# Cross-attention and two feed-forward layers in one kernel: the low half of an attention output tile taken by TensorE and ScalarE instead of VectorE

## The chip, the cores and the metric

The kernel runs on one NeuronCore of one Trainium2 chip. The metric is the device time of one execution in microseconds (us), the median of several runs. Five engines work side by side on one core: TensorE (PE in the profile, its weight loads PEld), VectorE (DVE), ScalarE (ACT), GpSimd (POOL) and SyncE (SP, which here only issues transfers). Each runs its own list of instructions in order, and they meet only at semaphores: a `wait_ge` on one engine blocks everything that is queued behind it on that engine.

## What is computed

The reference chains four blocks on 512 tokens (2 batches of 256) of width 512: a quantised product with the context, a mixture of 18 experts, a cross-attention with 32 heads on 8 key/value heads, and a gated low-rank layer. The change is in the cross-attention:

```python
q = (hidden_states @ q_proj_w.T).reshape(B, Q, NUM_HEADS, HEAD_DIM).transpose(0, 2, 1, 3)
...
scores = jnp.einsum('bhqd,bhkd->bhqk', q, k) * scale + attention_mask
attn = jax.nn.softmax(scores.astype(jnp.float32), axis=-1).astype(q.dtype)
out = jnp.einsum('bhqk,bhkd->bhqd', attn, v)
out = out.transpose(0, 2, 1, 3).reshape(B, Q, NUM_HEADS * HEAD_DIM)
return out @ o_proj_w.T
```

## The kernel before

**Numbers in two halves.** Every fp32 operand of a matrix product is held as two fp16 tensors, a high half (the value rounded to fp16) and a low half (the value minus the high half). `three_products` (L261 to L265) multiplies low by high, high by low and high by high into one PSUM bank, so each product of one 128-wide chunk is three matmuls of 128x512. Whoever produces an operand has to write both halves: typically ScalarE rounds (high) and GpSimd or VectorE subtracts (low).

**The attention stage.** The unit of work is a head tile `k`: one head, 128 query rows, 512 context columns. Four head tiles (`REP` = 4) that share one key/value head make an output tile `w` of 128 x 512, and four output tiles (`m` = 0 to 3) a group `g`; there are 8 groups (`KVH`), 32 output tiles and 128 head tiles. Each engine runs a function `attention(g, first)` over the 16 steps `j` of a group, once unrolled for group 0 and then as a hardware loop for groups 1 to 7:

- PE: `scores(k)` (3 matmuls) into one of the banks 0 to 3, having waited on `s_t` until head tile k-4 has left that bank; and in the same step one quarter of `values(w)` (3 matmuls) for the output tile three before, since its probabilities must have been exponentiated, normalised and transposed first. In group 0 there are values only in the last four steps. `values` writes into bank 6 or 7 by turns. At its first quarter it waits for the four transposes of its tile (`s_pT`) and, before the change, on `s_ol` until output tile w-2 has left the bank.
- DVE: `masked_scores` (L1374, PSUM to SBUF with the row maximum), `inverse_sum` of head tile k-1 (L1379), `prob_lo` of head tile k-2 (L1385, which waits for POOL's high half of the same tile), and once per output tile `o_lo` (L1390), the low half of the output, from PSUM and the high half.
- ACT: `exponentials` (L905), and once per output tile `o_hi` (L910), which rounds the output to fp16 into `q_sb`.
- POOL: `prob_hi` (L1092 on one column, then L1093 on 128x512), the high half of the probabilities. It waits for `inverse_sum` and, since the four slots of `hlr` are reused, for the transpose of head tile k-4.
- SP: `prob_transpose` (L325 to L331), one DMA transpose for each head tile, after `prob_lo`.

The order is written out by hand in these functions; there is no scheduler. After the loop PE finishes the values of output tiles 29, 30 and 31 with the output projection of group 0, `o_group(0)`, between the last two, and goes on with `o_group(1)` to `o_group(5)` and the last two projections.

`o_hi` and `o_lo` are what the change touches; before it they are

```python
def o_hi(w, mw):
    act.wait_ge(s_pv, w + 1)
    act.activation(q_sb[:, bass.ds(w, 1), 0, :], ps[6 + mw % 2][:, :], ACT.Copy, scale=1.0 / PSCALE).then_inc(s_oh, 1)
...
def o_lo(w, mw):
    dve.wait_ge(s_oh, w + 1)
    dve.scalar_tensor_tensor(out=q_sb[:, bass.ds(w, 1), 1, :], in0=ps[6 + mw % 2][:, :], scalar=1.0 / PSCALE,
                             in1=q_sb[:, bass.ds(w, 1), 0, :], op0=ALU.mult, op1=ALU.subtract).then_inc(s_ol, 1)
```

## Time and profile before

| | us |
|---|---|
| median of 3 runs | 716.15 (716.12 to 718.03) |
| the profiled execution | 715.52 |
| its span, first to last instruction | 713.7 |
| PE busy | 636.0 (89%) |
| DVE busy | 456.5 (64%) |
| POOL busy | 412.9 (58%) |
| ACT busy | 347.4 (49%) |
| granted TensorE clock, mean | 0.983 of full speed |

The span is shorter than the execution's time by 1.8 us that lie around it. Busy shares are means over stages with different limits: what bounds one stage is read from its own stretch of the trace. The attention stage lies between about 384 and 595 us of the span, the output projection and the last layer behind it.

### The profile page before, as it was taken

The numbers are of one execution on the slowest core, as the hardware profiler recorded it, in microseconds if no ns is written. First come the engines' busy times: TensorE is split into PE (matmuls) and PEld (weight loads), VectorE is DVE, ScalarE is ACT, GpSimd is POOL, SyncE is SP. The second block draws the span as 40 slices with busy tenths as digits, with TensorE's granted clock in tenths as the row PEclk, the third lists the DMA queues.
The fourth block names the chain that finished last, engine by engine and source line by source line (L and its number), as shares of the span: only waits on it lengthen the run. The fifth ranks groups of instructions, "written<-read, shape, count | busy, mean of one in ns | idle before, by whom it ended". The sixth has DMA issues, their size and how long they took to land.

```text
span 713.7 us, 12272 instructions
## 1 busy us (share of the span) xinstructions
PE 636.0 (89%) x3356; PEld 298.0 (42%) x3356; DVE 456.5 (64%) x1086; ACT 347.4 (49%) x706; POOL 412.9 (58%) x438
## 2 busy tenths in 40 slices
PE   5639999999999999999997778888888878999997
PEld 2214445444444444455553233333333333444453
DVE  5999886443444337544446999999999992000573
ACT  4415556533343323778777555565556552223122
POOL 4823233355455422677777878888888883538201
PEclk9959999999999999999999999999999999999999
DMA  8802000244444331121223998888888885134001
GB/s 328 336 0 74 1 0 0 91 133 147 132 124 138 120 133 60 60 104 74 90 86 93 168 166 163 161 162 162 162 162 161 162 162 121 59 118 176 1 1 60
DMA packets 149112, 83.04 MB, mean 116 GB/s; under 512 B 136762, under 2 KB 136890, under 8 KB 146141
## 3 DMA queue, kind: packets, MB, share of 16 engines
q1 hardware_dynamic: 146290, 77.90, 42.8%
q10 hardware_dynamic: 2795, 4.79, 2.2%
q8 instruction: 15, 0.25, 0.1%
q14 instruction: 12, 0.10, 0.0%
HBM read 48.03 MB, written 1.09 MB: 69 GB/s over the span
## 4 chain that ended last, share of the span: by engine, by line
PE 45%; DVE 20%; issue 17%; POOL 12%; DMA 2%; ACT 2%; DVEq 1%; POOLq 1%; SPq 0%; ACTq 0%
PE ps L263 15%; PE ps L265 14%; PE ps L264 14%; POOL hlr L1093 5%; POOL wsp L1013 4%; POOL hlr L1013 3%; DVE q_sb L1390 3%; DVE st L1136 1%; DVE f32r L1374 1%; PE ps L357 1%; DVE nw L1148 1%; DVE hlr L1385 1%; DVE nw L1147 1%; DVE f32r L1152 1%; DMA stage<-in_first_chunks 1%
## 5 line engine op out<-in xcount | busy, mean ns | idle before, releaser
L1013 POOL TENSOR_TENSOR wsp<-stage,wsp 128x512 f16<-128x512 f32 (+1 forms) x93 | 135.3, 1479 | 130.8 <-ACT wsp L744 68.5
L905 ACT ACTIVATE f32r<-f32r,mneg 128x512 f32<-128x512 f32 x128 | 92.4, 722 | 85.2 <-DVE mneg L1374 85.2
L1013 POOL TENSOR_TENSOR hlr<-f32r,hlr 128x512 f16<-128x512 f32 x52 | 61.2, 1178 | 100.0 <-ACT hlr L796 66.4
L1092 POOL TENSOR_SCALAR rinv<-rinv 128x1 f32<-128x1 f32 x128 | 83.1, 650 | 34.4 <-DVE rinv L1379 22.7
L1385 DVE SCALAR_TENSOR_TENSOR hlr<-f32r,rinv,hlr 128x512 f16<-128x512 f32 x128 | 95.6, 747 | 9.8 <-POOL hlr L1093 3.0
L1093 POOL TENSOR_SCALAR hlr<-f32r,rinv 128x512 f16<-128x512 f32 x128 | 92.7, 724 | 0.0
L1374 DVE CUSTOM_DVE_ANT_0 f32r<-ps,nmask 128x512 f32<-128x512 f32 x128 | 87.3, 683 | 0.0
L1293 DVE TENSOR_REDUCE ss<-f32r 128x4 f32<-128x512 f32 x48 | 32.9, 685 | 55.1 <-ACT f32r L785 55.0
L263 PE MATMUL ps<-q_sb 128*128 128x512 f16 x128 | 49.2, 385 | 9.0 <-POOL q_sb L1013 7.3
L1343 DVE SCALAR_TENSOR_TENSOR f32r<-ps,par,f32r 128x512 f32<-128x512 f32 x18 | 13.5, 751 | 66.3 <-PE ps L265 63.4
L263 PE MATMUL ps<-xT,wsp 128*128 128x512 f16 x144 | 55.3, 384 | 0.0
L264 PE MATMUL ps<-xT,wsp 128*128 128x512 f16 x144 | 55.1, 383 | 0.0
L265 PE MATMUL ps<-xT,wsp 128*128 128x512 f16 x144 | 55.1, 383 | 0.0
L263 PE MATMUL ps<-k_sb,q_sb 128*128 (+1 forms) x128 | 48.6, 380 | 3.8 <-DVE mneg L1374 3.5
L264 PE MATMUL ps<-q_sb 128*128 128x512 f16 x128 | 49.2, 385 | 0.0
L265 PE MATMUL ps<-q_sb 128*128 128x512 f16 x128 | 49.0, 383 | 0.0
L263 PE MATMUL ps<-wsp,xT 128*128 128x512 f16 x128 | 48.5, 379 | 0.1
L264 PE MATMUL ps<-k_sb,q_sb 128*128 (+1 forms) x128 | 48.5, 379 | 0.0
L265 PE MATMUL ps<-k_sb,q_sb 128*128 (+1 forms) x128 | 48.5, 379 | 0.0
L265 PE MATMUL ps<-wsp,xT 128*128 128x512 f16 x128 | 48.5, 379 | 0.0
L264 PE MATMUL ps<-wsp,xT 128*128 128x512 f16 x128 | 48.5, 379 | 0.0
L785 ACT ACTIVATE f32r<-ps 128x512 f32<-128x512 f32 x48 | 28.7, 597 | 39.5 <-PE ps L265 39.0
(228 smaller groups left out, 1361.8 us busy)
## 6 DMA issues: line engine op xcount, KB each, us to landing
stage<-in_moe SPq DMA_DIRECT2D x18, 512.0 KB, 3.5
stage<-in_wq SPq DMA_DIRECT2D x8, 1024.0 KB, 4.8
stage<-in_wo SPq DMA_DIRECT2D x8, 1024.0 KB, 4.8
stage<-in_moe SPq DMA_DIRECT2D x18, 256.0 KB, 3.2
hlr<-gates_dram ACTq DMA_DIRECT2D x18, 256.0 KB, 3.1
k_sb<-in_wkv SPq DMA_DIRECT2D x3, 1024.0 KB, 18.7
stage<-in_first_chunks SPq DMA_DIRECT2D x4, 512.0 KB, 6.1
q_sb<-in_ctx_nat SPq DMA_DIRECT2D x1, 2048.0 KB, 14.9
```

What stands on the lines that cost most here:

```text
L263: pe.matmul(dst, lhs[0], rhs[1], start=start, stop=False, skip_group_check=True)
L264: pe.matmul(dst, lhs[1], rhs[0], start=False, stop=False, skip_group_check=True)
L265: return pe.matmul(dst, lhs[0], rhs[0], start=False, stop=stop, skip_group_check=True)
L785: act.activation(f32r[:, j % 2, :], ps[j % 4][:, :], ACT.Square).then_inc(s_sq, 1)
L905: act.activation(f32r[:, j % 4, :], f32r[:, j % 4, :], ACT.Exp, bias=mneg[:, j % 4:j % 4 + 1], scale=-1.0, accum_out=psum_col[:, j % 4:j % ...
L1013: return pool.tensor_tensor(dst_lo, src, dst_hi, ALU.subtract)
L1092: pool.tensor_scalar(rinv[:, 1, j % 4:j % 4 + 1], rinv[:, 0, j % 4:j % 4 + 1], PSCALE, None, ALU.mult)
L1093: pool.tensor_scalar(hlr[:, j % 4, 0, :], f32r[:, j % 4, :], rinv[:, 0, j % 4:j % 4 + 1], PSCALE, ALU.mult, ALU.mult).then_inc(s_ph, 1)
L1293: dve.tensor_reduce(ss[:, j % 2, :], f32r[:, j % 2, :].rearrange("p (h d) -> p h d", h=REP), AX_X, ALU.add).then_inc(s_ss, 1)
L1374: dve.tensor_tensor_reduce(f32r[:, j % 4, :], ps[j % 4][:, :], nmask[:, qt, :], 0.125, BIG, ALU.add, ALU.min, mneg[:, j % 4:j % 4 + 1]).th ...
L1385: dve.scalar_tensor_tensor(out=hlr[:, j % 4, 1, :], in0=f32r[:, j % 4, :], scalar=rinv[:, 1, j % 4:j % 4 + 1], in1=hlr[:, j % 4, 0, :], op ...
L1390: dve.scalar_tensor_tensor(out=q_sb[:, bass.ds(w, 1), 1, :], in0=ps[6 + mw % 2][:, :], scalar=1.0 / PSCALE, in1=q_sb[:, bass.ds(w, 1), 0, ...
```

## The change

The low half of an output tile is no longer computed on VectorE. PE multiplies the fp16 high half by a new constant matrix `negid`, minus `PSCALE` (16384) times the identity, and accumulates that onto the same PSUM bank, so that the bank then holds `PSCALE` times the difference; ACT evicts the bank a second time into the low half. The bank is busy longer for it, and the values get four banks (4 to 7) instead of two. The wait of `values` on `s_ol` now asks for output tile w-4 instead of w-2 (the semaphore's start value goes from 1 to 4 accordingly). `residual` of output tile w-4 stands in PE's step 2 of 4 of each output tile, between scores and values, and waits for `o_hi` (`s_oh`); `o_lo` stands in ACT's step 3 of 4 and waits for `residual` (`s_or`). `negid` is made once, at the start, by one more VectorE instruction.

```diff
@@ PE @@
-                        pe.wait_ge(s_ol, w)
-                par = mw % 2
+                        pe.wait_ge(s_ol, w + 1)
                 last = three_products(
-                    pe, ps[6 + par][:, :],
+                    pe, ps[4 + mw][:, :],
...
+            def residual(w, mw):
+
+                pe.wait_ge(s_oh, w + 1)
+                pe.matmul(ps[4 + mw][:, :], negid[:, :], q_sb[:, bass.ds(w, 1), 0, :],
+                          start=False, stop=True, skip_group_check=True).then_inc(s_or, 1)
+
             def attention(g, first):
...
                         scores(g, j, k, first)
+                    if c == 2 and not first:
+                        residual(4 * g + m - 4, m)
                     if not first or m >= 3:
                         values(4 * g + m - 3, g if m >= 3 else g - 1, (m - 3) % 4, c, not first)
...
             for w in (1, 2):
                 for c in range(SC):
                     values(4 * (KVH - 1) + w, KVH - 1, w, c)
+                residual(4 * (KVH - 1) + w - 1, w - 1)
             o_group(0, 0, True)
+            residual(4 * KVH - 2, 2)
             for c in range(SC):
                 values(4 * KVH - 1, KVH - 1, 3, c)
 
             o_group(1, 1, False)
+            residual(4 * KVH - 1, 3)
...
-            pe.wait_ge(s_ol, 1 + 4 * KVH)
+            pe.wait_ge(s_ol, 4 + 4 * KVH)
@@ ACT @@
             def o_hi(w, mw):
                 act.wait_ge(s_pv, w + 1)
-                act.activation(q_sb[:, bass.ds(w, 1), 0, :], ps[6 + mw % 2][:, :], ACT.Copy, scale=1.0 / PSCALE).then_inc(s_oh, 1)
+                act.activation(q_sb[:, bass.ds(w, 1), 0, :], ps[4 + mw][:, :], ACT.Copy, scale=1.0 / PSCALE).then_inc(s_oh, 1)
+
+            def o_lo(w, mw):
+                act.wait_ge(s_or, w + 1)
+                act.activation(q_sb[:, bass.ds(w, 1), 1, :], ps[4 + mw][:, :], ACT.Copy, scale=1.0 / PSCALE).then_inc(s_ol, 1)
...
                     if hh == 0 and not first:
                         o_hi(4 * g + m - 4, m)
+                    if hh == 3 and not first:
+                        o_lo(4 * g + m - 4, m)
...
-            o_hi(4 * KVH - 4, 0)
-            o_hi(4 * KVH - 3, 1)
-            o_hi(4 * KVH - 2, 0)
+            for m in range(2):
+                o_hi(4 * KVH - 4 + m, m)
+                o_lo(4 * KVH - 4 + m, m)
+            o_hi(4 * KVH - 2, 2)
...
-            o_hi(4 * KVH - 1, 1)
+            o_lo(4 * KVH - 2, 2)
+            o_hi(4 * KVH - 1, 3)
...
+            o_lo(4 * KVH - 1, 3)
@@ DVE @@
+            dve.tensor_scalar(negid[:, :], ident[:, :], -PSCALE, None, ALU.mult)
...
-            dve.tensor_scalar(nmask[:, :, :], nmask[:, :, :], -8.0, None, ALU.mult).then_inc(s_ol, 1)
+            dve.tensor_scalar(nmask[:, :, :], nmask[:, :, :], -8.0, None, ALU.mult).then_inc(s_ol, 4)
...
-            def o_lo(w, mw):
-                dve.wait_ge(s_oh, w + 1)
-                dve.scalar_tensor_tensor(out=q_sb[:, bass.ds(w, 1), 1, :], in0=ps[6 + mw % 2][:, :], scalar=1.0 / PSCALE,
-                                         in1=q_sb[:, bass.ds(w, 1), 0, :], op0=ALU.mult, op1=ALU.subtract).then_inc(s_ol, 1)
...
-                    if hh == 1 and not first:
-                        o_lo(4 * g + m - 4, m)
...
-            for m in range(4):
-                o_lo(4 * KVH - 4 + m, m)
```

**On PE, inside the loop**, steps 2 and 3 of an output tile's first quarter of the loop body. In the rows a line number is that of the helper (`three_products`), `ps2<-k_sb,q_sb` is `scores` into bank 2, `ps7<-xT,v_sb` is `values` into bank 7 (its transposed probabilities lie in `xT`). Before:

```order
L576 REGISTER_ALU
L263 ISA [waits s_t]
L263 MATMUL ps2<-k_sb,q_sb 128x512
L264 ISA
L264 MATMUL ps2<-k_sb,q_sb 128x512
L265 MATMUL ps2<-k_sb,q_sb 128x512
L263 ISA
L263 MATMUL ps7<-xT,v_sb 128x512
L264 ISA
L264 MATMUL ps7<-xT,v_sb 128x512
L265 MATMUL ps7<-xT,v_sb 128x512
```

And now (all line numbers below the new declarations are 2 higher):

```order
L265 MATMUL ps2<-k_sb,q_sb 128x512
L266 ISA
L266 MATMUL ps2<-k_sb,q_sb 128x512
L267 MATMUL ps2<-k_sb,q_sb 128x512
L601 REGISTER_ALU
L602 ISA [waits s_oh]
L602 MATMUL ps4<-q_sb,negid 128x512
L265 ISA
L265 MATMUL ps5<-xT,v_sb 128x512
L266 ISA
L266 MATMUL ps5<-xT,v_sb 128x512
L267 MATMUL ps5<-xT,v_sb 128x512
```

The residual matmul and its wait on ACT's high half stand behind the scores of that step and in front of its values; everything PE does later is queued behind this wait. The values' bank is 5 instead of 7.

**On ACT, inside the loop**, one output tile: four exponentials (`f32r,psum_col<-f32r,mneg`), one `o_hi` behind the first, before:

```order
L905 ACTIVATE f32r,psum_col<-f32r,mneg 128x512 [waits s_t]
L909 REGISTER_ALU
L910 ISA [waits s_pv]
L910 ACTIVATE q_sb<-ps6 128x512
L904 REGISTER_ALU
L905 ACTIVATE f32r,psum_col<-f32r,mneg 128x512 [waits s_t]
L904 REGISTER_ALU
L905 ACTIVATE f32r,psum_col<-f32r,mneg 128x512 [waits s_t]
L904 REGISTER_ALU
L905 ACTIVATE f32r,psum_col<-f32r,mneg 128x512 [waits s_t]
```

And now, from the third exponential of one tile to the `o_hi` of the next:

```order
L917 ACTIVATE f32r,psum_col<-f32r,mneg 128x512 [waits s_t]
L916 REGISTER_ALU
L917 ACTIVATE f32r,psum_col<-f32r,mneg 128x512 [waits s_t]
L926 ISA [waits s_or]
L926 ACTIVATE q_sb<-ps5 128x512
L916 REGISTER_ALU
L917 ACTIVATE f32r,psum_col<-f32r,mneg 128x512 [waits s_t]
L921 REGISTER_ALU
L922 ISA [waits s_pv]
L922 ACTIVATE q_sb<-ps6 128x512
```

The second eviction stands behind the fourth exponential, so two evictions now stand behind two exponentials in a row.

**On ACT, behind the loop**, the last output tiles and the casts of the weights for `o_group(1)` (`wsp<-stage`). Before:

```order
L910 ACTIVATE q_sb<-ps6 128x512 [waits s_pv]
L910 ACTIVATE q_sb<-ps7 128x512 [waits s_pv]
L910 ACTIVATE q_sb<-ps6 128x512 [waits s_pv]
L933 DMA k_sb<-in_l_wq 128x64
L933 DMA k_sb<-in_l_keys 16x64
L886 CAST wsp<-stage 128x512 [waits s_w1]
L886 CAST wsp<-stage 128x512 x3
L910 ACTIVATE q_sb<-ps7 128x512 [waits s_pv]
```

And now:

```order
L922 ACTIVATE q_sb<-ps4 128x512 [waits s_pv]
L926 ACTIVATE q_sb<-ps4 128x512 [waits s_or]
L922 ACTIVATE q_sb<-ps5 128x512 [waits s_pv]
L926 ACTIVATE q_sb<-ps5 128x512 [waits s_or]
L922 ACTIVATE q_sb<-ps6 128x512 [waits s_pv]
L952 DMA k_sb<-in_l_wq 128x64
L952 DMA k_sb<-in_l_keys 16x64
L898 CAST wsp<-stage 128x512 [waits s_w1]
L898 CAST wsp<-stage 128x512 x3
L926 ACTIVATE q_sb<-ps6 128x512 [waits s_or]
L922 ACTIVATE q_sb<-ps7 128x512 [waits s_pv]
```

Two evictions that wait for a residual product of PE have moved in front of the weight casts.

## Rows read from the trace of the kernel before

**Rows 1.** The page, busy time of each engine.
```profile
PE 636.0 (89%) x3356; PEld 298.0 (42%) x3356; DVE 456.5 (64%) x1086; ACT 347.4 (49%) x706; POOL 412.9 (58%) x438
```

**Rows 2.** Stretches: length, busy us (count) by engine, PEclk, DMA share, GB/s.
```profile
391.00:407.00 16.00, 12.84 (x52) 4.55 (x53) 15.10 (x44) 8.44 (x21) 14.71 (x21) 1.00 0.91 170
...
430.00:455.90 25.90, 21.40 (x97) 9.32 (x96) 24.88 (x69) 14.96 (x37) 21.69 (x33) 1.00 0.85 162
...
592.76:665.20 72.44, 72.44 (x336) 32.85 (x337) 2.09 (x5) 20.86 (x40) 40.41 (x36) 1.00 0.31 108
```

**Rows 3.** Waits of the whole span: us in total, times, longest.
```profile
PE ps L263 <- DVE q_sb L1390: 34.8, 28, 3.6
```

**Rows 4.** Timeline, one output tile and a later DVE row: start, us, engine, line, [idle before].
```profile
449.71 0.68 DVE L1390 SCALAR_TENSOR_TENSOR q_sb<-ps,q_sb 128x512 f32 x1
450.31 0.68 DVE L1374 CUSTOM_DVE_ANT_0 f32r<-ps,nmask 128x512 f32<-128x512 f32 x1
450.64 0.39 PE L263 MATMUL ps<-wsp,v_sb 128*128 128x512 f16 x1 [1.24 <-DVE q_sb L1390]
453.89 0.72 ACT L905 ACTIVATE f32r<-f32r,mneg 128x512 f32<-128x512 f32 x1 [0.70 <-DVE mneg L1374]
454.61 0.57 ACT L910 ACTIVATE q_sb<-ps 128x512 f32 x1
...
475.60 0.68 DVE L1390 SCALAR_TENSOR_TENSOR q_sb<-ps,q_sb 128x512 f32 x1
```

**Rows 5.** Timeline of DVE in group 0, where no output is evicted.
```profile
397.72 0.75 DVE L1385 SCALAR_TENSOR_TENSOR hlr<-f32r,rinv,hlr 128x512 f16<-128x512 f32 x1
398.38 0.68 DVE L1374 CUSTOM_DVE_ANT_0 f32r<-ps,nmask 128x512 f32<-128x512 f32 x1
```

**Rows 6.** Timeline of POOL in group 0, two steps in a row.
```profile
398.51 0.69 POOL L1093 TENSOR_SCALAR hlr<-f32r,rinv 128x512 f16<-128x512 f32 x1
...
400.03 0.69 POOL L1093 TENSOR_SCALAR hlr<-f32r,rinv 128x512 f16<-128x512 f32 x1
```

**Rows 7.** L330's transposes in 391:403, then 430:580, then 405:418.
```profile
DMA to landing us min/median/max: 3.1/3.4/3.7
...
DMA to landing us min/median/max: 3.0/3.3/3.6
...
DMA to landing us min/median/max: 3.1/3.6/5.0
```

**Rows 8.** The chain that ended last, around the start of group 1: start, us, what.
```profile
402.27 0.76 DVE hlr L1385
...
403.53 3.32 DMA pT<-hlr
...
412.58 4.99 DMA wsp<-hlr
```

**Rows 9.** Timeline of POOL, the step that waited for the first of these transposes.
```profile
407.02 0.62 POOL L1092 TENSOR_SCALAR rinv<-rinv 128x1 f32<-128x1 f32 x1 [0.23 <-DMA pT<-hlr]
```

**Rows 10.** Timeline of DVE: head tiles 16 and 127's masks, and tile 123's low half.
```profile
407.50 0.68 DVE L1374 CUSTOM_DVE_ANT_0 f32r<-ps,nmask 128x512 f32<-128x512 f32 x1
...
584.95 0.75 DVE L1385 SCALAR_TENSOR_TENSOR hlr<-f32r,rinv,hlr 128x512 f16<-128x512 f32 x1
...
587.55 0.68 DVE L1374 CUSTOM_DVE_ANT_0 f32r<-ps,nmask 128x512 f32<-128x512 f32 x1
```

**Rows 11.** Timeline of PE behind the loop: values of tile 30, then `o_group(0)`.
```profile
592.76 0.38 PE L263 MATMUL ps<-pT,v_sb 128*128 128x512 f16 x1 [3.56 <-DVE q_sb L1390]
...
595.35 0.38 PE L263 MATMUL ps<-wsp,q_sb 128*128 128x512 f16 x1
```

**Rows 12.** Timeline of DVE in the first stage, on four columns.
```profile
16.90 0.79 DVE L1142 TENSOR_SCALAR nw<-mv 128x4 f32<-128x4 f32 x1
```

**Rows 13.** Timeline of PE, and the stretch around it, at the lower clock.
```profile
44.56 1.89 PE L501 MATMUL ps<-xT,pT 128*128 128x512 f16 x4 [1.08 <-DVE v_sb L1187]
...
41.00:45.00 4.00, 2.31 (x18) 1.80 (x19) 3.97 (x5) 2.08 (x3) 0.00 (x0) 0.50 0.00 0
```

More of the change, by code:

```diff
@@ L79, in xattn_ffn_kernel @@
         ident = sb("ident", [P, P], F16)
+        negid = sb("negid", [P, P], F16)
         par = sb("par", [P, PAR_END], F32)
@@ L231, in xattn_ffn_kernel @@
         s_oh = sem("s_oh")
+        s_or = sem("s_or")
         s_ol = sem("s_ol")
```

## The prediction

> **What bounds the kernel now.** I read the page first, for the busy shares [rows 1]: PE leads with 89%, DVE has 64%. These are means, so I cut the span into stretches [rows 2]. Behind the attention loop, from 592.76 us, PE is busy for all of 72.44 us with 336 matmuls: 0.2156 us each, PE-bound. Inside the loop (430 to 455.9) PE is busy for 21.4 of 25.9 us, DVE for 24.9, POOL for 21.7 and ACT for 15.0. The view of waits says what PE waits for: DVE's low half of an output tile, 28 times, 34.8 us [rows 3]. That sum is not what the change gains. The timeline shows why: four evictions by L1390 lie from 449.71 to 475.60 apart [rows 4], so an output tile takes 6.47 us, and within that time DVE hardly ever rests. PE's wait is slack that it has because DVE is slower.
>
> What sets DVE's pace is seen where nothing is evicted, in group 0. There POOL's L1093 recurs every 1.52 us [rows 6], while DVE's L1385 is followed by L1374 after 0.66 us [rows 5]. L1385 of 397.72 ends at 398.47, L1093 starts at 398.51: 0.04 us later. L1093 ends at 399.20, and the next L1385 waits for it. The two alternate: 0.75 + 0.04 + 0.69 + 0.03 = 1.51 us for each head tile, whatever else DVE does. DVE's L1374 (0.68, reading PSUM) fits in beside L1093. In the loop before, one L1390 per output tile adds 0.60 us (449.71 to 450.31 [rows 4]), during which POOL gets on, so the next step is shorter than 1.52: 6.47 - 3 x 1.517 - 0.60 = 1.32 is left for it.
>
> **DVE, the loop: 28 evictions go.** An output tile then costs 4 x 1.517 = 6.07 us instead of 6.47, a gain of 0.40. Not 0.60, because POOL's turn becomes the limit again. 28 output tiles: **-11.3 us**.
>
> **PE, one matmul more.** 25 x 0.2156 = 5.39 us per output tile, under 6.07, so hidden. But PE now waits for ACT's high half with the rest of its list behind it. Counted from the end of the mask of the tile's first head (the instant that frees its exponential): ACT begins the exponential 0.04 later, begins o_hi 0.72 after that and takes 0.57 (L905 and L910 in [rows 4]): 1.33. PE wakes up 0.25 later (L1390's end at 450.39 to the matmul at 450.64 [rows 4]), and needs 7 matmuls (one residual, three of values, three of scores) and 0.17 until the last is written (a matmul shows 0.39 where they follow every 0.22): 3.3 us. DVE wants these scores, three head tiles on, at 3 x 1.517 - 0.68 = 3.9. So 0.6 us of slack, and DVE is not starved; PE gains 0.22 us per head tile on it until the next residual. Cost 0.
>
> **ACT, one eviction more.** An exponential and an eviction take 0.72 + 0.57 = 1.29, under 1.52 even in two steps in a row. By the time of the fourth exponential the residual is long done. Cost 0, and 0.23 us of cover for each such step.
>
> **PSUM banks.** The wait for output tile w-4, two tiles older than before, asks for something done long ago: 0. It is what takes the 34.8 us of PE's waits away; most come back as PE waiting for DVE or for o_hi, about 6.07 - 5.39 = 0.68 per tile.
>
> **The transposes.** POOL's L1092 for head tile k waits for the transpose of k-4. From L1385's end at 403.03 to L1092 at 407.02 it takes 3.99 us with a landing of 3.32 [rows 8, 9], so 0.67 beside the landing; L1092 needs 0.2, then L1093 0.69, 0.03, L1385 0.75. A round of four head tiles takes the landing + 2.33. With 3.3 that is 5.65, under 6.07; it decides from a landing of 3.74. Landings are 3.1 to 3.7 at group 0's pace and 3.0 to 3.6 in the loop [rows 7], so the margin is thin but holds. Around the start of group 1 they reach 4.99 [rows 8]; before, the 0.60 of an L1390 covered part of that. Bounds: nothing more, or all of 4.99 - 3.74 = 1.25, twice. I take the one seen once at its full size less the 0.4 that it costs already (from head tile 16's mask to tile 127's it takes 180.05 us [rows 10], where 27 output tiles of 6.47 and three last steps of 5.0 in all make 179.7): **+0.9 us**, ends 0 and 2.1.
>
> The DMA engines' busy share at group 0's pace is 0.91 with 170 GB/s [rows 2], 1.38 us of all of them for each transpose: the pace of 1.52 is near what they take. The Trainium skill (Advanced Engine Details and Errata, X-Bar Transpose) expects 350 to 400 GB/s of a transpose. By that figure, an estimate, one would need about 0.7 us and the landing could not matter; by the row it can. The row decides, and that is why slower transposes are two of the rivals.
>
> **Behind the loop.** Let X be the end of the last head tile's mask, 588.24 [rows 10]. Before, PE waited 3.56 us for o_lo of tile 28, which DVE had behind its last probabilities, and began o_group(0) at 595.35, X + 7.1 [rows 11]. Now: the residual of tile 27 is done by X - 4.55 + 1.33 + 0.25 + 0.22 = X - 2.75, then nine matmuls to X - 0.8, values of tile 29 (12 matmuls, 2.59) to X + 1.8, residual 28 to X + 2.0, values of tile 30 to X + 4.6, residual 29 to X + 4.8. The transposes of tile 30 were landed by then: L1385 of head tile 123 ended at 585.70 [rows 10], without the L1390 between at X - 2.2, and 3.99 more is X + 1.8. So o_group(0) begins 2.3 us earlier relative to X. PE is the bound from there on, so residuals 30 and 31 cost their 2 x 0.22: **-1.9 us** in all. The weight casts for o_group(1) now stand behind residual 29 on ACT, but that group begins only 48 + 1 + 12 matmuls after X + 4.8, at X + 18, and they have those 13 us: no cost. Ends of this term: 0 (PE waits for something else) and -2.5.
>
> **The start.** `negid` is one 128x128 operation, like L1176, some 0.15 us on DVE. DVE then soon blocks, as POOL does behind L1385: L1142, on 4 columns, takes 0.79 us [rows 12], where a free instruction of that kind can't need it (L1374 has 0.68 for 512 columns). So the delay is taken up there: 0; ends 0 and 0.2.
>
> Sum: -11.3 + 0.9 - 1.9 = -12.3 us. On the profiled execution, 715.52, that gives 703.2. The median is 0.63 above the profiled execution, so **703.8 us**. The case's own range, from the ends above, is 702 to 707.
>
> **The rivals.**
> - *Transposes slow the loop somewhat.* With mean landings of 3.8 to 4.1 the round is 6.13 to 6.43 and the gain 0.34 to 0.04 per tile: 705 to 713. For it: the share of 0.91 and the landings of 4 to 5 around 410. Against: eleven head tiles of group 0 ran at 1.52 with no growth. Chance 0.11.
> - *Transposes make it slower than before.* The same ring at 4.99 as the usual landing: 7.32 per output tile, 28 x 0.85 = +24, less 1.9: 738. It decides from a mean landing of 4.14 (a round of 6.47). In the steady loop the longest landing was 3.6 [rows 7]. Chance 0.04.
> - *PE starves DVE.* If the chain mask, exponential, o_hi, residual, scores takes over 3.9 us, each 0.1 beyond adds 0.1 per tile. At 4.2 most of the gain is gone: 28 x 0.1, and 1.9, so 711; at 4.3 and beyond 714 and more. It needs handovers worth 0.6 more than those of [rows 4]. Chance 0.04.
> - *Nothing is won behind the loop* (transposes or casts late there): 705.7. Chance 0.05, inside the range.
> - *The alternation does not bind*, DVE goes at 1.33 and PE at 5.39 per tile is the bound: 28 x 1.08 + 1.9 = 32, so 684. Against it: group 0 has no L1390 and does not go faster than 1.52. Chance 0.02.
> - *The clock falls.* In the loop PE idles 1.24 us per tile [rows 4] at a granted clock of 1.00 [rows 2], the level of 2.4 GHz; the new idling is shorter and the share of PE greater. At 0.50, the level of 1.2 GHz, a 512-column matmul takes 0.43 us (four in 1.89, the last one shown with 0.6 [rows 13]), 10.7 us per output tile, and the kernel some 120 us more: about 830. The Trainium skill (TensorE: Matmul & The Clock Gate, A second HAM failure mode) describes a kernel that cycles through PSUM banks and whose small idle times between groups of matmuls make the clock swing, which four banks in turn and a wait per tile resemble; this trace, with more idling, does not show it. Chance 0.01.
>
> **The numbers.** The forecast has 0.73. A measurement of this kernel can tell about 0.3%, 2.1 us. Faster by more: forecast, no gain behind the loop, the unbound case and nearly all of the first rival, 0.92 with some of the starving case. Within 0.3%: 0.03. Slower: 0.05. The range reaches from 701 to 709 and leaves out 0.16: the slower transposes, PE starving DVE, the clock, the unbound case, and the upper half of the first rival.
>
> **What would show it.** In the changed profile: no L1390; L1093 every 1.52 us through all groups; 24.3 us instead of 25.9 for four output tiles; DVE's rests only behind POOL; PE waiting for ACT's o_hi some 0.7 us per tile and hardly for DVE's L1390; o_group(0) 4.8 us after the last mask. I am wrong if POOL waits for DMA in the loop, if DVE waits for PE's scores, or if the steps are not 1.52.

## The result and the profile after

The changed kernel takes **700.79 us** (median of 4 runs, 699.88 to 701.52) against 717.03 us of the kernel before on the same chip (716.12 to 718.03): ratio 0.9773, 95% interval 0.9751 to 0.9794. Forecast were 703.8 us and a range of 701.0 to 709.0. The direction and the bottleneck are as forecast; the time lies just under the range, 3 us below the forecast, and the sizes of two terms are off.

| us | before | after |
|---|---|---|
| the profiled execution | 715.52 | 699.88 |
| its span | 713.7 | 698.0 |
| start of head tile 16's mask | 407.50 | 405.61 |
| start of head tile 127's mask | 587.55 | 573.61 |
| between the two (the loop) | 180.05 | 168.00 |
| the first mask of the attention stage | 382.45 | 380.52 |

Lines moved in the file: the mask L1374 is now L1396, the reciprocal L1379 is L1401, the low half of the probabilities L1385 is L1407, POOL's L1092 and L1093 are L1113 and L1114, the high half of the output L910 is L922, and the three products stand in L265 to L267. New are L602 (the residual on PE) and L926 (ACT's second eviction). The page's busy times [rows 1]: PE and ACT are busy for 9.6 and 15.7 us more, DVE for 18.1 us less.

```profile
PE 645.6 (92%) x3388; PEld 302.6 (43%) x3388; DVE 438.4 (63%) x1055; ACT 363.1 (52%) x738; POOL 410.5 (59%) x438
```

The stretch of the loop that [rows 2] show, in the changed kernel (length, busy us (count) for PE, PEld, DVE, ACT, POOL, then PEclk, DMA share, GB/s), and the four microseconds after the first residual:

```profile
430.00:455.90 25.90, 24.05 (x110) 10.43 (x108) 24.50 (x69) 18.19 (x43) 23.20 (x35) 1.00 0.92 174
...
408.00:412.00 4.00, 4.00 (x12) 1.52 (x12) 3.49 (x9) 2.44 (x7) 2.95 (x6) 0.57 0.92 181
```

DVE is still the busiest engine, and nearly all of its rest is behind POOL; POOL went from 21.7 to 23.2 us of 25.9, and PE from 21.4 to 24.05. In 408:412 PE's granted clock is 0.57 on average; the profile of the kernel before has 1.00 there.

The waits between 387 and 575 us (total in us, times, longest) that answer to [rows 3], which had PE waiting for DVE's eviction: PE's 34.8 us behind DVE are gone, and 15.0 us behind ACT's high half have come.

```profile
PE ps L602 <- ACT q_sb L922: 15.0, 26, 3.6
...
DVE hlr L1407 <- POOL hlr L1114: 6.0, 29, 0.9
...
POOL rinv L1113 <- DMA pT<-hlr: 0.9, 2, 0.8
DVE f32r L1396 <- issue: 0.8, 1, 0.8
```

The timeline of DVE and POOL in the steady loop (start, us, engine, line, [idle before]), two steps that are not alike. DVE's masks and reciprocals, which lie between, are left out here:

```profile
439.58 0.75 DVE L1407 SCALAR_TENSOR_TENSOR hlr<-f32r,rinv,hlr 128x512 f16<-128x512 f32 x1
439.65 0.75 POOL L1113 TENSOR_SCALAR rinv<-rinv 128x1 f32<-128x1 f32 x1
440.38 0.69 POOL L1114 TENSOR_SCALAR hlr<-f32r,rinv 128x512 f16<-128x512 f32 x1
441.17 0.21 POOL L1113 TENSOR_SCALAR rinv<-rinv 128x1 f32<-128x1 f32 x1
441.20 0.75 DVE L1407 SCALAR_TENSOR_TENSOR hlr<-f32r,rinv,hlr 128x512 f16<-128x512 f32 x1 [0.18 <-POOL hlr L1114]
441.35 1.16 POOL L1114 TENSOR_SCALAR hlr<-f32r,rinv 128x512 f16<-128x512 f32 x1
442.55 0.75 DVE L1407 SCALAR_TENSOR_TENSOR hlr<-f32r,rinv,hlr 128x512 f16<-128x512 f32 x1
```

The first step is the one of the forecast: POOL's small L1113 comes just behind DVE's product, is held up until that ends (0.75 us for one column), and L1114 begins 0.05 after it. The second is another: L1407 starts 0.13 us after L1114's end (441.07) instead of 0.04, L1113 is done before in 0.21 us, and L1114 stands issued already while DVE's product runs. It ends at 442.51, 0.56 us after DVE's product (441.95) instead of 0.74 (440.33 to 441.07). The two steps take 1.62 + 1.35 = 2.97 us instead of 3.03. In the loop this comes once in every output tile and sometimes twice: at slot 0 DVE's list has a register to compute (16 times the number of the output tile, the value of its second wait) between the two waits of `prob_lo`.

The Trainium skill (SBUF — State Buffer, Who interferes with whom) says that a DVE instruction with two inputs in SBUF and a GpSimd instruction that reads SBUF exclude each other, and that the order of issue decides who blocks. The rows agree: DVE's L1407 reads two tensors of SBUF and alternates with L1114, while L1396 reads PSUM and one tensor of SBUF and runs beside it. An L1114 that is issued while DVE's product still runs ends 0.18 us sooner after it than one that is issued later (0.56 against 0.74); that is what the two steps show.

At the start of group 1 PE came to the first residual long before ACT had evicted output tile 0, and the matmuls behind it soon ran at the low clock; behind the loop it goes as forecast (timeline of PE at both places, and of DVE at the mask that had to wait for scores):

```profile
407.80 0.39 PE L602 MATMUL ps<-q_sb,negid 128*128 x1 [3.63 <-ACT q_sb L922]
...
408.76 0.63 PE L265 MATMUL ps<-k_sb,q_sb 128*128 x1
...
412.60 0.69 DVE L1396 CUSTOM_DVE_ANT_0 f32r<-ps,nmask 128x512 f32<-128x512 f32 x1 [0.80 <-issue]
...
579.00 0.38 PE L602 MATMUL ps<-q_sb,negid 128*128 128x512 f16 x1
579.21 0.38 PE L265 MATMUL ps<-wsp,q_sb 128*128 128x512 f16 x1
```

The last mask starts at 573.61 and ends at 574.30, so `o_group(0)` begins 4.91 us after it (forecast 4.8; before 7.11 [rows 10, 11]). From there to the end it takes 118.79 us instead of 118.35: the two residuals, 0.44.

The sum between the two profiles: 1.93 before the attention stage, less 0.04 in group 0, 12.05 in the loop, 2.20 between the last mask and `o_group(0)`, less 0.44 = **15.70 us**, as the spans differ. Forecast were 0, 0, 10.4, 2.3 and 0.43, in all 12.3. So 1.93 stand in a place where the forecast had nothing, and 1.65 in the loop.

### The profile page after: what moved, and what is told of

Its sections match the earlier page's. It is cut to its first block, busy times and chain, and to the rows that moved or that the text cites. A ratio compares the mean times of both kernels' runs of the same rounds, so it can differ in the third digit from the quotient of the medians.

```text
span 698.0 us, 12345 instructions
## 1 busy us (share of the span) xinstructions
PE 645.6 (92%) x3388; PEld 302.6 (43%) x3388; DVE 438.4 (63%) x1055; ACT 363.1 (52%) x738; POOL 410.5 (59%) x438
## 4 chain that ended last, share of the span: by engine, by line
PE 43%; DVE 19%; issue 18%; POOL 15%; ACT 2%; DMA 1%; SPq 1%; DVEq 1%; POOLq 1%; ACTq 0%
PE ps L265 14%; PE ps L267 14%; PE ps L266 14%; POOL hlr L1114 8%; POOL wsp L1034 4%; POOL hlr L1034 3%; DVE f32r L1396 3%; DVE st L1157 1%; PE ps L359 1%; DVE nw L1169 1%; DVE nw L1168 1%; DVE f32r L1173 1%; DVE hlr L1407 1%; DMA stage<-in_first_chunks 1%; DVE xT L1232 1%
## 5 line engine op out<-in xcount | busy, mean ns | idle before, releaser
L1114 POOL TENSOR_SCALAR hlr<-f32r,rinv 128x512 f16<-128x512 f32 x128 | 105.1, 821 | 0.0
L1407 DVE SCALAR_TENSOR_TENSOR hlr<-f32r,rinv,hlr 128x512 f16<-128x512 f32 x128 | 96.0, 750 | 12.2 <-POOL hlr L1114 7.1
L1396 DVE CUSTOM_DVE_ANT_0 f32r<-ps,nmask 128x512 f32<-128x512 f32 x128 | 87.5, 684 | 0.8 <-issue 0.8
L1113 POOL TENSOR_SCALAR rinv<-rinv 128x1 f32<-128x1 f32 x128 | 68.9, 538 | 24.2 <-DVE rinv L1401 15.0
L265 PE MATMUL ps<-q_sb 128*128 128x512 f16 x128 | 49.6, 387 | 9.1 <-POOL q_sb L1034 7.3
L265 PE MATMUL ps<-xT,wsp 128*128 128x512 f16 x144 | 54.6, 379 | 0.0
L266 PE MATMUL ps<-xT,wsp 128*128 128x512 f16 x144 | 54.6, 379 | 0.0
L267 PE MATMUL ps<-xT,wsp 128*128 128x512 f16 x144 | 54.6, 379 | 0.0
L265 PE MATMUL ps<-k_sb,q_sb 128*128 (+1 forms) x128 | 49.8, 389 | 2.3 <-DVE mneg L1396 2.1
L267 PE MATMUL ps<-q_sb 128*128 128x512 f16 x128 | 49.5, 387 | 0.0
L266 PE MATMUL ps<-k_sb,q_sb 128*128 (+1 forms) x128 | 49.4, 386 | 0.0
L267 PE MATMUL ps<-k_sb,q_sb 128*128 (+1 forms) x128 | 49.3, 385 | 0.0
L265 PE MATMUL ps<-wsp,xT 128*128 128x512 f16 x128 | 48.5, 379 | 0.1
L267 PE MATMUL ps<-wsp,xT 128*128 128x512 f16 x128 | 48.5, 379 | 0.0
```

What stands on the lines that cost most here:

```text
L265: pe.matmul(dst, lhs[0], rhs[1], start=start, stop=False, skip_group_check=True)
L266: pe.matmul(dst, lhs[1], rhs[0], start=False, stop=False, skip_group_check=True)
L267: return pe.matmul(dst, lhs[0], rhs[0], start=False, stop=stop, skip_group_check=True)
L1113: pool.tensor_scalar(rinv[:, 1, j % 4:j % 4 + 1], rinv[:, 0, j % 4:j % 4 + 1], PSCALE, None, ALU.mult)
L1114: pool.tensor_scalar(hlr[:, j % 4, 0, :], f32r[:, j % 4, :], rinv[:, 0, j % 4:j % 4 + 1], PSCALE, ALU.mult, ALU.mult).then_inc(s_ph, 1)
L1396: dve.tensor_tensor_reduce(f32r[:, j % 4, :], ps[j % 4][:, :], nmask[:, qt, :], 0.125, BIG, ALU.add, ALU.min, mneg[:, j % 4:j % 4 + 1]).th ...
```

## Experiments

"Tiles" below are the times from the mask of head tile 4w to that of 4w+4, read as differences of the mask's starts on the timeline of DVE; "the loop" is from head tile 16's mask to 127's.

### Is it the banks, or DVE's eviction?

`banks_alone` is the kernel before with this edit:

```diff
-                        pe.wait_ge(s_ol, w)
-                par = mw % 2
+                        pe.wait_ge(s_ol, w + 1)
-                    pe, ps[6 + par][:, :],
+                    pe, ps[4 + mw][:, :],
...
-            dve.tensor_scalar(nmask[:, :, :], nmask[:, :, :], -8.0, None, ALU.mult).then_inc(s_ol, 1)
+            dve.tensor_scalar(nmask[:, :, :], nmask[:, :, :], -8.0, None, ALU.mult).then_inc(s_ol, 4)
...
+            pe.wait_ge(s_t, 16 * KVH)
             o_group(0, 0, True)
```

> The kernel before with four value banks in turn, the low half still on DVE; PE waits for the last mask before o_group(0), which the eviction order gave it before. If PE's 34.8 us of waiting for the low half were slack that DVE's slower pace gave it: an output tile stays at 6.47 us, PE waits for DVE's masks instead, and only the 2 to 2.5 us behind the loop are gained: 714 to 715.5 us. Rival: the wait for the bank was on the path. Then most of the loop's gain comes with the banks alone, an output tile near 6.0 to 6.1 us, and the time is 701 to 705 us.

Measured: 713.34 us (711.01 to 713.98), ratio 0.9964 (0.995 to 0.9978) to before. The steady output tile stays at 6.47 us and the loop at 179.49 us. PE's waits between 387 and 590 us are now these, and behind the loop `o_group(0)` starts at 590.82, 4.88 us after the last mask's end (585.26 + 0.68 = 585.94):

```profile
PE ps L263 <- DVE mneg L1374: 18.6, 32, 0.7
PE ps L263 <- DMA pT<-hlr: 3.3, 1, 3.3
```

The 34.8 us of waiting were slack, as the prediction said. Four banks alone shorten the part behind the loop (7.11 to 4.88 us from the last mask to `o_group(0)`) and change nothing in it. The 4.88 hold a stretch at the low clock, which the changed kernel does not have there: behind a stop of 3.28 us the twelve matmuls of output tile 30 take 3.87 us instead of 2.59 (timeline of PE, first of them and first of `o_group(0)`):

```profile
586.95 0.59 PE L263 MATMUL ps<-pT,v_sb 128*128 128x512 f16 x1 [3.28 <-DMA pT<-hlr]
...
590.82 0.38 PE L263 MATMUL ps<-wsp,q_sb 128*128 128x512 f16 x1
```

At the full clock it would be 3.6 (by the matmuls' times, an estimate), so the banks give more there than the changed kernel gets; that its residuals take some of it back is likely, as `low_out_four_banks` below has 3.97 there without them and at the full clock. That 4.88 is so near the changed kernel's 4.91 is chance. The time fell a little more than expected.

`low_out_two_banks` and `low_out_four_banks` leave out the low half of the output tiles: the first takes `o_lo` out of DVE in the kernel before, the second takes the residual products and ACT's second evictions out of the changed one; PE's wait for a free bank goes by `s_oh`. The second also has PE wait for the last mask before `o_group(0)`, as `banks_alone` does.

```diff
-                        pe.wait_ge(s_ol, w)
+                        pe.wait_ge(s_oh, w)
...
-                    if hh == 1 and not first:
-                        o_lo(4 * g + m - 4, m)
```

```diff
-                        pe.wait_ge(s_ol, w + 1)
+                        pe.wait_ge(s_oh, w + 1)
...
-                    if c == 2 and not first:
-                        residual(4 * g + m - 4, m)
...
-                    if hh == 3 and not first:
-                        o_lo(4 * g + m - 4, m)
```

> The kernel before without the low half of the output tiles (what stands there stays what it was), on two banks; PE waits for ACT's high half of two tiles ago. DVE has nothing but its share of the head tiles. If DVE's eviction alone made the difference: an output tile 6.0 to 6.06 us, head tile 16 to 127 in 168 to 170 us, and no residual behind the loop: 700 to 701 us. Rival: two banks hold PE up as soon as DVE is faster; then an output tile above 6.1 us and 703 us or more.

> The changed kernel without its residual products and second evictions (the low half is left out), PE waiting for nothing of them. If both are hidden in the loop, only the two residuals behind it go, 2 x 0.22: 700.3 us, an output tile 5.99 to 6.06 us. Rival: PE's wait for ACT's high half (15 us in 26 waits) or the start of group 1, where PE's clock falls, is paid for by the residuals: then 1 to 3 us less, 697.5 to 699.5 us, with a shorter fifth and seventh output tile (6.99 and 6.67 us in the changed kernel).

Measured: 699.56 us (697.26 to 701.17), ratio 0.9771 (0.9735 to 0.9808), and 699.35 us (697.24 to 699.61), ratio 0.9764 (0.9733 to 0.9796). Their loops take 167.23 and 167.10 us, with steady tiles of 5.93 to 6.00 and 5.86 to 6.08. So it is DVE's eviction that set the loop's pace; how many banks there are changes nothing there. Against the changed kernel's 168.00 the residuals and second evictions cost 0.9 us in the loop, as the second expectation's rival had it: 0.6 of it in the first five tiles (31.61 against 31.04), and 0.01 a tile in the rest. In the same four microseconds after the first evictions PE's clock is not lowered:

```profile
408.00:412.00 4.00, 3.79 (x17) 1.54 (x16) 3.44 (x12) 2.84 (x7) 2.88 (x7) 1.00 1.16 178
```

### Why 5.99 us and not 6.07 for an output tile?

`one_wait_low_prob` is the changed kernel without the second wait of `prob_lo` (POOL makes it for the same head tile before its high half, so it says nothing new):

```diff
                 dve.wait_ge(s_ph, k + 1)
-                if earlier is not None:
-                    dve.wait_ge(s_pT[j % 4], 16 * earlier)
```

> The changed kernel with prob_lo waiting for POOL's high half alone; the second wait (that the transpose is done) is already made by POOL for the same head tile. No register is computed between POOL's end and the start of DVE's product any more. Theory A (a late start of this product, by 0.1 us once per output tile, lets POOL's small scaling slip in ahead and makes the next step 1.35 us): all steps become 1.517 us, an output tile 6.07 instead of 5.99, 28 x 0.08 = 2.2 us slower than the changed kernel: about 703 us. Theory B (the shorter output tile has another cause, and a wait taken away can only help): 700 to 701 us.

Measured: 701.36 us (700.95 to 701.77), ratio 0.9792 (0.9767 to 0.9816). The median (701.36) lies between what the two theories give and does not decide; the profile does. Every step is 1.515 us (L1407 is L1405 here), L1113 takes 0.75 each time, and the loop is 169.61 us instead of 168.00 (405.88 to 575.49):

```profile
438.56 0.75 DVE L1405 SCALAR_TENSOR_TENSOR hlr<-f32r,rinv,hlr 128x512 f16<-128x512 f32 x1
440.07 0.75 DVE L1405 SCALAR_TENSOR_TENSOR hlr<-f32r,rinv,hlr 128x512 f16<-128x512 f32 x1
441.59 0.75 DVE L1405 SCALAR_TENSOR_TENSOR hlr<-f32r,rinv,hlr 128x512 f16<-128x512 f32 x1
443.11 0.75 DVE L1405 SCALAR_TENSOR_TENSOR hlr<-f32r,rinv,hlr 128x512 f16<-128x512 f32 x1
```

The tiles are 6.05 to 6.06 behind the loop's first three: a wait taken away makes the loop 1.6 us longer. Theory A holds. 169.61 is also what the prediction's own numbers give for this distance (180.05 - 10.4 = 169.65), in part by luck: the tiles are 0.01 to 0.02 shorter than its 6.07, and the start of group 1 costs more than it said.

`late_low_prob` puts the late start into every step of the loop:

```diff
                     dve.wait_ge(s_pT[j % 4], 16 * earlier)
+                if not isinstance(k, int):
+                    dve.wait_ge(s_pl, 4 * earlier - j % 4)
```

> The changed kernel with one more wait, always met, before every product of prob_lo in the loop, on a register of its own, so that each of these products starts some 0.1 us (0.2 in one of four) after POOL's end. Theory A: from start to start 0.75 for the product, 0.56 until POOL's high half, issued already, is done, and 0.13 to 0.2: 1.44 to 1.47 us each step, an output tile 5.8 to 5.85, 4 to 6 us less than the changed kernel: 695 to 697 us. Theory B (DVE's path sets the pace, and a delay is a delay): 96 to 112 x 0.1 = 10 us more: 710 us.

Measured: 705.52 us (704.92 to 706.62), ratio 0.9853 (0.9827 to 0.988): between the two theories, and neither's. The steps alternate, 1.61 (437.76 to 439.37) and 1.43 (439.37 to 440.80), but in most tiles one of the long ones is 1.70; tiles of 6.07 to 6.39, 6.20 in the mean. Timeline of DVE (L1409 is the product) and POOL:

```profile
439.35 0.21 POOL L1113 TENSOR_SCALAR rinv<-rinv 128x1 f32<-128x1 f32 x1
439.37 0.75 DVE L1409 SCALAR_TENSOR_TENSOR hlr<-f32r,rinv,hlr 128x512 f16<-128x512 f32 x1 [0.17 <-POOL hlr L1114]
439.53 1.15 POOL L1114 TENSOR_SCALAR hlr<-f32r,rinv 128x512 f16<-128x512 f32 x1
440.80 0.75 DVE L1409 SCALAR_TENSOR_TENSOR hlr<-f32r,rinv,hlr 128x512 f16<-128x512 f32 x1
440.95 0.66 POOL L1113 TENSOR_SCALAR rinv<-rinv 128x1 f32<-128x1 f32 x1 [0.28 <-DVE rinv L1401]
```

After a step in which it slipped in ahead, POOL is so early that it has to wait for DVE's next reciprocal (0.28), which stands right before DVE's next product; its L1113 is then held up by that product again. The short step can't come twice in a row. What theory A had left out is that POOL's small operation itself waits for DVE; with that, the lateness costs 0.09 and more in each pair (1.61 against 1.52) and gives back 0.09 (1.43).

### Taking POOL's small operation away

If the held-up L1113 is what keeps L1114 from standing issued behind DVE's product, each step should be short without it. L1113 only multiplies the reciprocal by 16384. Three kernels leave it out. `unscaled` has no such factor at all in the probabilities and their products (negid and the evictions have 1), `unscaled_two_ops` is the same with POOL's form of two multiplications. The first has this edit:

```diff
-PSCALE = 16384.0
+PSCALE = 1.0
...
-                pool.tensor_scalar(rinv[:, 1, j % 4:j % 4 + 1], rinv[:, 0, j % 4:j % 4 + 1], PSCALE, None, ALU.mult)
-                pool.tensor_scalar(hlr[:, j % 4, 0, :], f32r[:, j % 4, :], rinv[:, 0, j % 4:j % 4 + 1], PSCALE,
-                                   ALU.mult, ALU.mult).then_inc(s_ph, 1)
+                pool.tensor_scalar(hlr[:, j % 4, 0, :], f32r[:, j % 4, :], rinv[:, 0, j % 4:j % 4 + 1], None,
+                                   ALU.mult).then_inc(s_ph, 1)
```

`unscaled_two_ops` has `PSCALE, ALU.mult, ALU.mult` in the last two lines. In both, DVE's product takes `rinv[:, 0, ...]` as its scalar.

> The changed kernel without the factor of 16384 on the probabilities: POOL's small scaling of the reciprocal goes, the high half is one multiplication, the evictions and negid have the factor 1. Theory A: POOL's high half is always issued while DVE's product holds it up, and ends 0.56 us behind it: 1.35 us a step by this pair, about 1.43 by DVE's own three operations (0.66 + 0.61 + 0.16), so an output tile 5.4 to 5.75 us, and group 0 faster too: 28 x 0.25 to 0.6 and 1 us: 690 to 693 us, unless the transposes bind (1.38 us each for all DMA engines, 5.5 per output tile). Theory B (the small operation isn't on the path): 700 to 701 us.

> As the run without the factor of 16384, but POOL's high half keeps its two multiplications (the second by 1), as in the changed kernel. Theory A: the 759 us of that run came from the form with one multiplication (1.7 us instead of 0.7 to 1.2); with two, and without the small scaling, a step is 1.35 to 1.43 us and the kernel takes 690 to 694 us. Theory B: without the small operation POOL issues two high halves in a row and DVE's product waits for both; then steps come in pairs, of 1.6 us each or more, and the kernel takes 705 us or more.

Measured: `unscaled` 759.32 us (ratio 1.0613, 1.0583 to 1.0644), a clear miss of both theories; `unscaled_two_ops` 691.37 us (690.79 to 692.13), ratio 0.9666 (0.9639 to 0.9693), as theory A said. The difference between them is the form of one instruction. The group of POOL's high half in `unscaled`, then in `unscaled_two_ops` (duration in ns, min/median/max):

```profile
L1113 POOL TENSOR_SCALAR hlr<-f32r,rinv x128: 1556/1560/1927, 384.2 to 635.9; 128x512 f16<-128x512 f32 x128
```

```profile
L1113 POOL TENSOR_SCALAR hlr<-f32r,rinv x128: 687/692/1238, 384.8 to 567.4; 128x512 f16<-128x512 f32 x128
```

With one multiplication POOL needs at least 1.56 us for the same tile, with two 0.69. With one multiplication the two engines don't take turns either: in `unscaled`, by the rows, DVE's product runs beside POOL's high half and takes 1.17 us instead of 0.75, so the exclusion described further up does not hold for this form (timeline of POOL and of DVE; POOL's two operations end at 387.26):

```profile
384.16 3.10 POOL L1113 TENSOR_SCALAR hlr<-f32r,rinv 128x512 f16<-128x512 f32 x2 [1.75 <-DVE rinv L1400]
385.76 1.17 DVE L1406 SCALAR_TENSOR_TENSOR hlr<-f32r,rinv,hlr 128x512 f16<-128x512 f32 x1 [0.59 <-POOL hlr L1113]
```

In `unscaled_two_ops` group 0 runs at 1.345 us a step (tiles of 5.38), which is 0.75 + 0.56 + 0.04, the short step of the changed kernel. It is also what DVE's own operations take there (product to mask 0.66, mask to reciprocal 0.61, reciprocal to product 0.07), so these rows don't tell which of the two holds the step. In the loop the tile is 5.5 to 5.9, 5.7 in the mean, and POOL waits for the transposes, in 445:470 with the DMA engines at 0.97 (timeline of POOL, then the stretch):

```profile
442.96 0.69 POOL L1113 TENSOR_SCALAR hlr<-f32r,rinv 128x512 f16<-128x512 f32 x1 [0.67 <-DMA xT<-hlr]
```

```profile
445.00:470.00 25.00, 24.37 (x111) 10.62 (x110) 24.55 (x72) 18.73 (x44) 12.52 (x18) 1.00 0.97 184
```

`act_scales_sum` keeps the factor and lets ACT bring it in, so that nothing is left out of the computation:

```diff
-                               accum_out=psum_col[:, j % 4:j % 4 + 1]).then_inc(s_e, 1)
+                               accum_out=psum_col[:, j % 4:j % 4 + 1]).then_inc(s_su, 1)
+                act.wait_ge(s_su, k + 1)
+                act.activation(rinv[:, 1, j % 4:j % 4 + 1], psum_col[:, j % 4:j % 4 + 1], ACT.Copy, scale=1.0 / PSCALE).then_inc(s_e, 1)
...
-                dve.reciprocal(rinv[:, 0, j % 4:j % 4 + 1], psum_col[:, j % 4:j % 4 + 1]).then_inc(s_r0, 1)
+                dve.reciprocal(rinv[:, 0, j % 4:j % 4 + 1], rinv[:, 1, j % 4:j % 4 + 1]).then_inc(s_r0, 1)
```

(POOL and `prob_lo` as in `unscaled_two_ops`, with 1.0 as the second factor.)

> The changed kernel with its factor of 16384 kept, but brought in by ACT: behind each exponential it multiplies the row sums by 1/16384, DVE takes the reciprocal of that, and POOL's small scaling is gone. If the pace is set as in the unscaled kernel: ACT's small operation costs 0.2 to 0.4 us in the chain exponential to reciprocal, which has about 0.5 us of slack, so 691 to 693 us. Rival: the chain gets too long, DVE's reciprocal waits for ACT in every head tile, a step is 1.5 us or more, and it takes 700 us or more.

Measured: **692.20 us** (691.69 to 693.0), ratio 0.9662 (0.9633 to 0.969): 8.6 us less than the changed kernel. The steady tile is 5.71 to 5.74, as in the unscaled kernel, but here it is not the transposes that hold it. Once per tile DVE's mask waits for PE's scores and starts 0.13 us after the last of them (timeline of PE, then of DVE):

```profile
445.06 0.38 PE L268 MATMUL ps<-k_sb,q_sb 128*128 x1
445.57 0.69 DVE L1398 CUSTOM_DVE_ANT_0 f32r<-ps,nmask 128x512 f32<-128x512 f32 x1
```

From 430 to 545 us, 20 tiles, DVE loses 6.5 us against its own 5.38 a tile: 4.0 before masks, 1.3 before reciprocals (for ACT's scaled sum) and 1.2 before products. The prediction's rival of PE starving DVE, which stayed away at 6.0 us a tile, is here at 5.7.

`before_act_scales_sum` is the same edit in the kernel before, which keeps DVE's eviction and its two banks.

> The kernel before (two banks, DVE's eviction) with the factor brought in by ACT as in the 692 us kernel, POOL's small scaling gone. In group 0 a step falls from 1.517 to some 1.38 us as it did there. In the loop DVE is busy nearly without rest: 4 x (0.66 + 0.61 + 0.16) + 0.60 = 6.32 us for an output tile by its own operations, instead of 6.47: 28 x 0.15 = 4.2, and 1.3 in group 0: 710.5 to 711.5 us against 716.3. If DVE were not the bound of the loop before, but the pair with POOL alone (POOL catching up 0.6 us in each output tile), the output tile would come down by the same 0.35 us as in the changed kernel or more, to 6.1, and the time to 705 us.

Measured: 702.55 us (701.83 to 704.04), ratio 0.9807 (0.9772 to 0.9842). The expectation was wrong: the tile falls from 6.47 to 6.00 (5.97 three times and 6.09), not to 6.3. Here DVE hardly ever rests, and the rows show what its own work takes (L1387 the product, L1376 the mask, L1392 the eviction):

```profile
449.51 0.75 DVE L1387 SCALAR_TENSOR_TENSOR hlr<-f32r,rinv,hlr 128x512 f16<-128x512 f32 x1
450.17 0.68 DVE L1376 CUSTOM_DVE_ANT_0 f32r<-ps,nmask 128x512 f32<-128x512 f32 x1
450.78 0.16 DVE L1381 RECIPROCAL rinv<-rinv 128x1 f32<-128x1 f32 x1
450.86 0.75 DVE L1387 SCALAR_TENSOR_TENSOR hlr<-f32r,rinv,hlr 128x512 f16<-128x512 f32 x1
451.52 0.68 DVE L1392 SCALAR_TENSOR_TENSOR q_sb<-ps,q_sb 128x512 f32 x1
452.12 0.68 DVE L1376 CUSTOM_DVE_ANT_0 f32r<-ps,nmask 128x512 f32<-128x512 f32 x1
```

A head tile costs DVE 1.35 us (449.51 to 450.86), not my 1.43, and the eviction 0.60: 4 x 1.35 + 0.60 = 6.0. So in the kernel before 0.5 us per output tile was DVE waiting for POOL, and either remedy alone, the eviction moved (5.99) or POOL's operation removed (6.00), brings nearly the same; both together stop at 5.72, at the next limit.

### The start of group 1

`residual_later` is the changed kernel with this edit, and `unscaled_residual_later` has it in the 691 us kernel (`unscaled_two_ops`):

```diff
-                    if c == 2 and not first:
+                    if c == 3 and not first:
                         residual(4 * g + m - 4, m)
```

> The changed kernel with the residual product one head tile later in PE's order (c == 3 instead of c == 2). Theory C: at the start of group 1 PE came early to the first residual, stood 3.63 us for ACT's high half, and its clock then was granted at 0.50 for some 3 us, so that DVE waited for scores (output tiles 5 to 7: 6.99 + 5.83 + 6.67 = 19.49 us; without residuals 18.95). One head tile later the stop is about 2.1 us, the clock stays at 1.00, the three output tiles take 18.9 to 19.1 us, PE's waits for ACT's high half (15.0 us) go almost entirely, and the steady output tile is 5.99 as before: 700.0 to 700.5 us. Theory D: the later residual makes ACT's second eviction late, and with it the exponentials behind it; then output tiles of 6.1 us and more: 703 us or more.

> The 691 us kernel (no factor of 16384, two multiplications) with the residual one head tile later. There output tiles 5 to 7 take 19.31 us, where the steady ones take 5.71 each by the transposes that POOL waits for: 2.2 us more than steady. Theory C gives back a part of it, 0.5 to 1.5 us: 690 to 691 us, with the steady tile unchanged at 5.71. Theory D: ACT's second eviction comes late at this shorter step: output tiles of 5.8 and more, 694 us or more.

Measured: 699.98 us (699.11 to 701.39), ratio 0.9768 (0.9736 to 0.98), and 690.67 us (690.59 to 692.26), ratio 0.9646 (0.9617 to 0.9676). Neither differs from its parent by more than the runs scatter. In the profiles the changed kernel's loop falls from 168.00 to 167.06 us, what the kernel without residuals has (167.10), with tiles 5 to 7 of 6.06 + 6.01 + 6.46 = 18.53. PE's first stop is 2.10 us, as expected, but its clock fell all the same (timeline of PE; stretch):

```profile
409.57 0.39 PE L602 MATMUL ps<-q_sb,negid 128*128 x1 [2.10 <-ACT q_sb L922]
```

```profile
410.00:412.00 2.00, 2.00 (x6) 0.76 (x5) 1.67 (x5) 1.34 (x4) 1.51 (x4) 0.50 1.10 226
```

So theory C is half right: the 0.9 us comes back, though not by keeping the clock up; that PE had written the scores of one more head tile before it stopped would explain it, but no run separates that. PE's waits for ACT did not go either, 12.1 us in 26 times instead of 15.0. In the unscaled kernel tiles 5 to 7 are 19.31 us both times: nothing comes back there. How the residual costs its part at the start of group 1 stays open.

### The 1.93 us before the attention stage

`before_again` is the kernel before, unchanged.

> The kernel before once more, with a profile. The first mask of the attention came at 382.45 us in its first profile and between 380.4 and 380.9 us in five other profiles, of kernels that differ behind that place. If the 1.9 us were a passing fall of TensorE's clock in the experts' stage (granted 0.83 from 130 to 140 us), this run has its first mask at 380.5 to 381 and its span is shorter by as much. If they belong to the kernel before, it is at 382.4 again, with 0.83 from 130 to 140.

Measured: one run, 714.61 us, span 712.8, first mask at 380.71. The two stretches of this run, and of the first profile of the same kernel, with PEclk as the third number from the end:

```profile
130.00:140.00 10.00, 10.00 (x47) 4.24 (x46) 5.03 (x6) 5.57 (x7) 3.28 (x2) 1.00 0.41 131
585.00:595.00 10.00, 6.45 (x24) 2.44 (x23) 4.50 (x10) 2.52 (x7) 3.71 (x6) 0.83 0.70 123
```

```profile
130.00:140.00 10.00, 10.00 (x40) 3.86 (x38) 4.29 (x4) 4.73 (x6) 3.28 (x2) 0.83 0.42 131
587.00:597.00 10.00, 6.44 (x31) 2.77 (x29) 5.59 (x11) 3.70 (x9) 4.00 (x6) 1.00 0.75 135
```

The lowered clock at 130 to 140 us does not belong to either kernel: of 14 profiled executions five have it, the first of the kernel before, `low_out_two_banks`, `before_act_scales_sum`, `low_out_four_banks` and `residual_later`, kernels of either kind that do the same work up to there. In these five the first mask comes between 382.3 and 382.9 us, in the other nine, with 1.00 in that stretch, between 380.4 and 381.1. But another fall appears in its place: behind the loop, where PE stands 3.55 us for DVE's low half, the matmuls of output tile 30 ran at the low clock in `before_again`, and `o_group(0)` began 8.58 us after the last mask instead of 7.11. So the span is only 0.9 us shorter, where the first theory expected 1.9: 1.80 less up to head tile 16's mask, 0.61 less in the loop (179.44), 1.47 more behind it. The same fall is in the profiles of `before_act_scales_sum`, which keeps that wait, and of `banks_alone`. The changed kernel has no such stop there, and none of the profiles with residuals shows the fall behind the loop.

## Why the prediction was right, and where it was wrong

**What bounds the kernel: right.** PE's 34.8 us of waiting were slack (`banks_alone`: all of it gone, the tile still 6.47), DVE's pace set the loop, and behind the eviction stood the alternation with POOL (`one_wait_low_prob`: 1.515 us in each step, 6.06 a tile).

**DVE's term, -11.3: the step that failed, undersized.** The prediction took the 1.517 of group 0 for every step, "because POOL's turn becomes the limit again". Measured is 5.99 us a tile, 0.08 under 6.07; over the loop's 27 tiles and three last steps the term is -13.4 instead of -11.3. In the changed kernel a register computed between two waits makes DVE 0.09 us late once per tile, POOL's small operation slips in ahead, and the next step is 1.35; without that wait every step is 1.515 (`one_wait_low_prob`). In group 0 the waits are against constants, so it is not seen there. The short step of the kernel before is another one, and there the prediction read the rows rightly: POOL's high half was done at 450.52, 0.47 us before DVE came to its product, so the order of the two did not matter (timelines of POOL and DVE):

```profile
449.83 0.69 POOL L1093 TENSOR_SCALAR hlr<-f32r,rinv 128x512 f16<-128x512 f32 x1
450.99 0.73 DVE L1385 SCALAR_TENSOR_TENSOR hlr<-f32r,rinv,hlr 128x512 f16<-128x512 f32 x1
```

**The start of group 1, +0.9: too small.** 27 tiles of 5.99 and three last steps of 4.65 in all make 166.3 of the loop's 168.00, so the start costs 1.7, where the kernel before had 0.3: +1.4. I had looked for the cost in the landings alone. They came as large as supposed (median 3.5, longest 4.9 between 403 and 418 us, 5.0 before [rows 7]) and POOL waited 1.1 us for them. Without residuals, in `low_out_four_banks`, the start costs 1.2, near the forecast's 0.4 + 0.9; the other 0.5 comes with the residual, which stopped PE for 3.63 us and was followed by a stretch at the low clock. The "0.6 us of slack" of the chain mask to scores was worked out at the full clock, and holds in the steady loop only (DVE waits for no scores there).

**Behind the loop, -1.9: right.** 4.91 instead of 4.8 us, and 0.44 for the residuals instead of 0.43: 1.76 in all. `banks_alone` shows that the banks bring it.

**PE, ACT, banks, start, all 0: right** in the steady loop (0.01 us a tile against `low_out_four_banks`); `negid` takes 0.19 us on DVE (0.15 supposed) and left no mark (first mask at 380.52, and at 380.71 in `before_again`).

**The base of the sum: no term for the clock's falls.** 1.93 us of the difference between the profiled executions are a passing fall of the clock in the profile that I worked from. I took one execution as the kernel's, added 0.63 to reach the median, and gave no width for such falls, though the runs shown spread over 1.9 us. The base itself, 716.15, was fair: four later sets of 7 to 13 runs of the kernel before have medians of 715.98 to 716.48. Without the 1.93 the terms measured in the two profiles come to 13.8 us, and with the loop of `before_again` to 13.2, which would give 702.4 to 703.0, inside the range. So the loop's terms alone do not explain that the median came out under it. The kernel before goes from 713.4 to 718.4 us over all its runs. How much of the remaining 2 us is that PE no longer stops behind the loop for DVE's low half (1.47 us where the clock falls) is left open; it would take the clock of many executions.

**The rivals.** Transposes as the limit: not at 6.0 (POOL waits 1.1 us for them in all), but at 5.7 in `unscaled_two_ops` they are. The round of landing + 2.33 had L1113 in it; without that it is 4.11 + 0.69 + 0.13 + 0.75 = 5.68 (from the product that ends at 438.85 to the high half at 442.96 it takes 4.11, and the next product starts at 443.78), and 5.7 was measured. PE starving DVE: not at 6.0, but at 5.7 in `act_scales_sum`. "The clock falls" came true for some 3 us at one place, not for the loop; the Trainium skill (TensorE: Matmul & The Clock Gate, A second HAM failure mode) describes such swings for matmuls that cycle through banks, while here the steady loop, with its stops of 0.43 us at a residual, keeps 1.00.
